# Second attention of a two-layer attention and expert program: the key-major scores from 32x128 stationary tiles

## What is computed

```
Q = query @ Wq + bq ; K = key @ Wk + bk ; V = value @ Wv + bv       (heads of 8 features)
Q = Q * cos + rotate_half(Q) * sin ; K = K * cos + rotate_half(K) * sin
scores = einsum('bhtd,bhsd->bhts', Q, K) / sqrt(8)
attn = softmax(scores, axis=-1)
context = einsum('bhts,bhsd->bhtd', attn, V) ; out = context @ Wo + bo
```

## Time and profile before

| | |
|---|---|
| median of 3 runs | 1782.54 us |
| lowest, highest | 1778.4, 1782.55 us |
| profiled execution, span from its first to its last instruction | 2270.0 us |
| a time of its own beside the span | the page gives none |
| busy: TensorE matmuls, VectorE, ScalarE, GpSimd | 1668.9, 1187.1, 941.9, 1124.3 us |
| mean granted TensorE clock | 0.830 |

### The profile page before, as it was taken

One profiled execution on the slowest core, in us unless ns is written; L12 is line 12 of the kernel. 1 busy time (PEld: TensorE's weight loads), 2 busy tenths in 40 slices (PEclk: granted clock), 3 DMA queues, 4 the chain that ended last, 5 costly groups with the idle time before them and its releaser, 6 DMA issues. The chain is left out here.

```text
span 2270.0 us, 58116 instructions
## 1 busy us (share of the span) xinstructions
PE 1668.9 (74%) x20814; PEld 1246.6 (55%) x20815; DVE 1187.1 (52%) x3485; ACT 941.9 (41%) x2258; POOL 1124.3 (50%) x1456
## 2 busy tenths in 40 slices
PE   6999993947877777826777767777855777777876
PEld 4777771437766677713444444444533555556654
DVE  5778777935555555623455455455666111222245
ACT  3777772723333333413334334344535233333322
POOL 4777761055555565464454454454212555555553
PEclk9999996967787777756888788778875898999888
DMA  4111110012323232521211111111000111111154
GB/s 169 44 42 36 41 30 13 1 44 77 82 77 79 77 85 78 75 59 63 84 41 37 34 40 36 34 39 37 24 14 15 37 40 37 41 40 40 39 143 140
DMA packets 136997, 122.89 MB, mean 54 GB/s; under 512 B 27675, under 2 KB 121915, under 8 KB 136123
## 3 DMA queue, kind: packets, MB, share of 16 engines
q0 software_dynamic: 26624, 56.35, 10.5%
q1 hardware_dynamic: 110078, 64.47, 9.3%
q10 hardware_dynamic: 192, 0.67, 0.1%
HBM read 80.24 MB, written 41.18 MB: 53 GB/s over the span
## 5 line engine op out<-in xcount | busy, mean ns | idle before, releaser
L1488 POOL DMA_INDIRECT arena<-expert_rows,token_of_slot x432 | 413.4, 957 | 402.0 <-issue 221.1
L419 POOL DMA_INDIRECT arena<-slot_results,slot x256 | 246.7, 964 | 118.5 <-issue 86.8
L1879 DVE TENSOR_TENSOR arena<-bank,arena 128x352 f32<-128x352 f32 x144 | 75.5, 524 | 354.3 <-ACT arena L1858 245.4
L1723 POOL DMA_INDIRECT token_results<-arena,slot x144 | 141.1, 980 | 189.9 <-DVE arena L1887 157.0
L909 PE MATMUL bank<-arena,Vp 128*32 128x64 f32 x4096 | 142.8, 230 | 114.6 <-issue 113.1
L1826 PE MATMUL bank<-W,arena 128*128 (+1 forms) x864 | 141.1, 305 | 108.9 <-ACT arena L1865 54.8
L1586 PE MATMUL bank<-arena 128*128 128x128 f32 x1152 | 195.7, 338 | 30.3 <-ACT arena L1633 12.7
L1826 PEld LDWEIGHTS bank<-W,arena 128*128 128x128 f32 (+1 forms) x864 | 127.2, 213 | 164.2 <-issue 156.7
L1812 PE MATMUL bank<-W,arena 128*128 x576 | 214.8, 500 | 1.7 <-ACT arena L1870 1.7
L1586 PEld LDWEIGHTS bank<-arena 128*128 128x128 f32 x1152 | 183.9, 249 | 39.7 <-issue 39.6
L619 DVE RECIPROCAL arena<-bank 128x256 f32<-128x256 f32 x64 | 112.1, 1752 | 173.6 <-PE bank L915 173.6
(11 more groups left out here) (215 smaller groups left out, 3622.8 us busy)
## 6 DMA issues: line engine op xcount, KB each, us to landing
slot_results<-arena SPq DMA_DIRECT2D x72, 256.0 KB
arena<-in_ctx SPq DMA_DIRECT2D x64, 128.0 KB
expert_rows<-arena SPq DMA_DIRECT2D x64, 128.0 KB
arena<-token_results SPq DMA_DIRECT2D x32, 256.0 KB
arena<-expert_rows,token_of_slot POOLq DMA_INDIRECT x432
W<-in_w SPq DMA_DIRECT2D x4, 1032.0 KB
X<-in_x SPq DMA_DIRECT2D x32, 128.0 KB, 2.1
arena<-slot_results,slot POOLq DMA_INDIRECT x256
```

The costliest lines, as they stand in the source:

```text
L419: nc.gpsimd.indirect_dma_start(out=gb[i.par][:, to:to + D], out_offset=None, in_=ys, in_offset=bass.IndirectOffsetOnAxis(ap=slot[:, at, k: ...
L1488: nc.gpsimd.indirect_dma_start(out=XE[n % R][:, c * ROW:(c + 1) * ROW], out_offset=None, in_=ts, in_offset=bass.IndirectOffsetOnAxis(ap=to ...
L1723: nc.gpsimd.indirect_dma_start(out=yt[half], out_offset=bass.IndirectOffsetOnAxis(ap=row_of_slot[:, at:at + 1], axis=0), in_=YE[n % 4][:, ...
```

## The change

In the second attention `turned` is replaced by `turned_pairs`. The block-diagonal keys, which exist already for `scores`, become the stationary operand: 32x128 tiles, two heads at once over all 128 output partitions, and 64 columns of the plain queries are the moving operand. This is again 32 matmuls. The maxima are subtracted by 32x128 slices of `max_to`, 256 columns of `mxT` as before, in 8 matmuls where there were 16. `Qbd` is no longer made or waited for. The first attention keeps `turned`; there, only conditions on `layer` that were always true or false are dropped.

```
-            Kbd, Qbd = carve2(1024), carve2(1024)
+            Kbd, Qbd = carve2(1024), None if layer else carve2(1024)
...
                             act.wait_ge(s["rope"], i.n + 1)
-                            for dst, src, done in ((Kbd, Kt, "kbd"), (Qbd, Qt, "qbd")):
-                                for j in range(4):
-                                    last = nc.scalar.activation(
-                                        dst[i.par].rearrange("p (b j k) -> p b j k", b=4, j=4)[:, :, j, :],
-                                        src[i.par].rearrange("p (b k) -> p b k", b=4), ACT.Copy,
-                                        scale=head_of[:, j:j + 1])
-                                last.then_inc(s[done], 1)
+                            for j in range(4):
+                                last = nc.scalar.activation(
+                                    Kbd[i.par].rearrange("p (b j k) -> p b j k", b=4, j=4)[:, :, j, :],
+                                    Kt[i.par].rearrange("p (b k) -> p b k", b=4), ACT.Copy,
+                                    scale=head_of[:, j:j + 1])
+                            last.then_inc(s["kbd"], 1)
...
+                    def turned_pairs(i):
+
+                        for sq in range(4):
+                            for j in range(2):
+                                for r in range(UNITS):
+                                    rows = slice(32 * r, 32 * r + 32)
+                                    nc.tensor.matmul(
+                                        U_[r][:, 128 * sq + 64 * j:128 * sq + 64 * j + 64],
+                                        Kbd[i.par][rows, 256 * sq + 128 * j:256 * sq + 128 * j + 128],
+                                        Qt[i.par][rows, 64 * sq:64 * sq + 64],
+                                        start=sq == 0 and j == 0, stop=False, skip_group_check=True)
+                        hold(pe, s["mx_here"], i.g + 1)
+                        for j in range(2):
+                            for r in range(UNITS):
+                                rows = slice(32 * r, 32 * r + 32)
+                                last = nc.tensor.matmul(
+                                    U_[r][:, :].rearrange("p (t j q) -> p t j q", t=4, j=2)[:, :, j, :],
+                                    max_to[rows, 2 * j * S:2 * (j + 1) * S],
+                                    mxT[rows, :].rearrange("p (t q) -> p t q", t=4),
+                                    start=False, stop=True, skip_group_check=True)
+                                if j == 1:
+                                    last.then_inc(s["t_psum"], 1)
...
                         if on(0):
                             maxima(i)
-                            turned(i)
+                            turned_pairs(i)
```

More of the change, by code:

```diff
@@ L869, in turned @@
                         hold(pe, s["qbd"], i.g + 1)
[L870 to L874, removed]
+                        for r, u in tiles_rb:
+                            rows = slice(32 * r, 32 * r + 32)
+                            nc.tensor.matmul(U_[r][64 * u:64 * u + 64, :], Mk[i.par][rows, 0:S], sel_of[rows, :],
+                                             start=True, stop=False, skip_group_check=True)
                         for sq in range(4):
@@ L883, in turned @@
                                     .rearrange("p (j u q) -> p j u q", j=2, u=2)[:, :, u, :],
-                                    start=bool(layer) and sq == 0, stop=False, skip_group_check=True)
+                                    start=False, stop=False, skip_group_check=True)
                         hold(pe, s["mx_here"], i.g + 1)
```

## The result

The changed kernel takes 1802.59 us (median of 4, 1797.48 to 1809.1) against 1782.55 us: a ratio of 1.0113, 95% interval 1.0083 to 1.0143. It is slower, by 20 us where 14 were forecast, and inside the range.

What follows compares the result with a forecast made beforehand. GpSimd was taken to bound gather steps at 13.1 us; the VectorE and TensorE loop would grow from 12.69 to 13.55, +0.45 times 27 = 12.2 us, plus 1.7 in closing steps: total +14, 1796 us, range 1777 to 1814.

Steps and rivals of the forecast that it cites:

- The pace of the wide tile: Key-major scores: 128-column load no longer hides under 64 moving columns; 16 x 0.110 = 1.76 us in place of 0.95.
- the ends of 0.94 and 2.70: Bounds for the wide scores group in us: load fully hidden, no change (0.94), or load and stream in turn (2.70).
- rival 3: Wide scores take load and stream in turn: 2.70 us, +1.75 a step, 1825 us in all; chance 0.07.
- The subtraction: Maxima subtracted after the scores: 16 instructions on four tiles keep the path's 1.1 us, change 0, bounds -0.1 and +0.1.
- the sum: Loop of VectorE and TensorE grows by 0.86 us, from 12.69 to 13.55; total +14 us.
- ScalarE's saving: Four Qbd activations fewer, -1.65 us of ScalarE's time: covered in gather steps, up to -0.28 us in closing steps.
- The bound of before: Gather steps of the second attention: GpSimd sets the step, by 0.4 us over the loop of VectorE and TensorE.
- The base of 13.1 us: Length taken for a gather step in the runs before the change; ends of 12.69 and 13.34 us.
- the closing steps: Five steps behind the last gather: 0.86 - 0.24 - 0.28 = +0.34 us each, 1.7 us in all.
- The lower clock: At 1.2 GHz 128 moving columns need as long as the load, so no cost; chance 0.22 together with rival 1.
- Against the profiled execution: Separate sum on the profiled span of 2270.0 us: 27 x (0.86 - 0.24) + 1.7 = +18, 2288 us.
- the standstill: TensorE idle in the values (L909) while GpSimd issues gathers; taken as in the profiled execution and mostly not the runs.

Runs made afterwards that it cites:

- b0: The kernel before, unchanged, run again for a second profile: 1784.13 us, ratio 0.9997.
- e5: The kernel before with only the subtraction of the maxima made wide (8 matmuls of 32x128), scores still narrow: 1780.97 us, ratio 0.9996.
- e6: The kernel before with the eight narrow score matmuls of the last sequence made twice: 1784.52 us, ratio 1.001.
- e9: The changed kernel with 96 of the 128 stationary columns in each score tile: 1792.65 us, ratio 1.0073.
- after: The changed kernel itself and its profile, against the kernel before: 1802.59 us, ratio 1.0113.
- e8: The changed kernel with 128 instead of 64 columns moving through each wide score tile: 1799.05 us, ratio 1.0102.
- e4: The changed kernel with the block-diagonal keys taken as 32x64 tiles (64 matmuls of 64 moving columns) and a narrow subtraction: 1808.14 us, ratio 1.0152.
- e3: The changed kernel with the subtraction of the maxima in the old narrow tiles (16 matmuls of 32x64): 1808.21 us, ratio 1.013.
- e7: The changed kernel with the wide score matmuls of the last sequence made twice: 1821.92 us, ratio 1.0229.
- e1: The changed kernel with Qbd still made by ScalarE and read by nobody: 1802.14 us, ratio 1.0091.
- e2: The kernel before with its narrow tiles but without Qbd, the block-diagonal keys read in its place: 1783.41 us, ratio 0.999.
- v1: The kernel before with GpSimd's two small products per step taken by ScalarE as four small activations: 1773.64 us, ratio 0.9963.
- v2: The kernel before with GpSimd's two small products and VectorE's copy of the gate logits both moved to ScalarE: 1773.59 us, ratio 0.996.

## Why the prediction was right, point by point

The mechanism held. Two of its sizes did not, and they partly cancelled, so that the forecast came closer than its terms. The table has, for each run, the distance from the start of the key-major scores to that of the projections, and the length of a step (from one L638 to the next), both as means from about 1000 to 1260 us, without the steps at a low granted clock and, for b0's distance, without the step of the late gather.

| run | two groups, us | step, us |
|---|---|---|
| b0 | 2.15 | 13.07 |
| e5, wide subtraction alone | 2.25 | 13.09 |
| e6, narrow group and a quarter | 2.44 | 13.28 |
| e9, 96 columns | 2.44 | 13.28 |
| after | 2.86 | 13.72 |
| e8, 128 columns moving | 2.86 | 13.71 |
| e4, 32x64 tiles of 64 columns | 2.98 | 13.85 |
| e3, wide scores, narrow subtraction | 2.99 | 13.84 |
| e7, wide group and a quarter | 3.31 | 14.15 |

From e6 on the step grows by what the two groups grow, whatever makes them longer: they lie on the loop that sets it. Above that, b0 and e5 stand at 13.07 and 13.09, where GpSimd holds the step.

- **The pace of the wide tile** was the step that decided: 16 x 0.110 = 1.76 us and 0.05 for the first load, 1.81 together, measured 1.84. Not the ends of 0.94 and 2.70. e8 excludes load and stream in turn (rival 3), e9 a fixed pace per tile. A rule that weight loads overlap only matmuls of another row group (the Trainium skill, "TensorE: Matmul & The Clock Gate", Part 3) would have made e8 27 us slower than after; it was not slower at all.
- **The subtraction** at 0: in the gather steps it was not. The projections start 1.03 us behind it in after and 1.15 in b0, and the narrow scores take 1.00 us there and not the 0.95 of a closing step. So the loop grew by 0.71 us where the sum had 0.86. Why the narrow groups vary from step to step was not tried. A change of width between the two groups costs 0.10 us (e3) or more (e5), a term that the sum did not have and did not need, because both groups have the same width.
- **ScalarE's saving** at nothing in gather steps: e1 and e2, from both sides.
- **The bound of before** was GpSimd: in b0 others wait for it and it waits for nobody. The base of 13.1 us was right (13.07), but its lead over the other loop was forecast at 0.4 us and is about 0.1: v1, with GpSimd out of the way, takes 12.96, and e6 gets 0.21 of its 0.29 us to show. The loop of VectorE and TensorE had been put at 12.69.
- **Sizes.** 0.86 added less 0.4 covered was 0.45 a step; 0.71 less some 0.1 is 0.65, as measured (13.72 - 13.07). Times 27 and with 0.8 for the closing steps (forecast 1.7) that is 18 us against 14. The profiled second attention has only 14.9 us, as good as the forecast, and that is luck: two of b0's steps stand at a low granted clock and are 3.8 us longer together, and none of after's is. The steps of after alternate: one with a wait of L852 of 0.77 us, the next with 0.58. The program's loop holds two steps, so its turn falls into every second; that this is the cause was not tried.
- **The 20 us of the medians**, with 18 from the steps, leave little open. Single executions of the changed kernel differ by more: 1797.48, 1799.67, 1805.51 and 1809.1 us, at mean granted clocks of 0.927, 0.928, 0.922 and 0.918, so the longer ones have the lower clock. Low stretches in the steps could do it (1.6 us each in e7), but this is not shown: e1's profiled execution is 4.9 us longer than after's with none, and 4.3 of them have passed before the first L638 (896.6 against 892.3). Nor do the profiles say what brings the stretches on. Between 1000 and 1300 us after, e1 and e8 have none, with the wide group; e7 has six, e9 five and e3 two; e4 has none; of the kernels with the narrow scores b0 has two, e2 and e5 one, and e6, v1 and v2 none.
- **The lower clock** the forecast had named only as a case in which the change would cost nothing. b0's narrow group at 0.50 bears that out for the group itself: 1.76 us to the subtraction, eight in sequence at 0.22 us each. That is the length of two wide loads, not of one as the forecast had it, which comes to the same, because the wide tiles are 16 in sequence. But a clock that falls for a few us also stretches the groups behind, in either kernel.
- **Against the profiled execution** the sum gave 2288 us, built on the standstill. The profiled execution after had none, so this number cannot be tested.

## What to carry to other kernels

In these groups a float32 matmul costs the longer of its stream and its weight load, as long as the number of instructions is not the limit (e4). With 64 moving and 128 stationary columns the load is the longer (0.115 against 0.059 us), and halving the stream while doubling the load was a loss even at the same number of instructions. Before pricing a change on one loop, look for an engine that never waits while others wait for it: here it was GpSimd, which hid about 0.1 us a step. Read the old length of a group in several steps of the stage that counts, not in one: here a single closing step gave 0.95 + 1.1 where the mean of the others was 2.15. When a profiled execution is much longer than the runs, look for a stretch that the runs cannot contain and take another profile before trusting its waits.

## What the runs showed of the hardware that was not expected

- The granted clock falls for a few us in the midst of steps of the unchanged kernel too. In b0 (a window as in e7's, and TensorE's timeline in it) it is 0.50, the lower level (1.2 of 2.4 GHz), and the narrow group then takes nearly as long as the wide one at the full clock, 1.76 us against 1.84:

```profile
1100.60:1104.00 3.40, 3.40 (x98) 2.57 (x96) 2.54 (x4) 0.69 (x3) 2.94 (x5) 0.50 0.15 39
```

```profile
1100.70 2.01 PE L878 MATMUL bank<-arena 32*64 32x128 f32 x64
1102.46 1.83 PE L890 MATMUL bank<-arena,fixed 32*64 32x256 f32 x32
```

- Narrow tiles with short streams (e4) do not come under 0.014 us for a load and its matmul over the whole group, so 128 of them took 1.80 us where loads and streams, as estimated for e4, would have allowed 0.9.
- Passing from 32x128 to 32x64 tiles between two groups of matmuls cost 0.10 us (e3), and from narrow to wide 0.09 to 0.22 (1.14 us in e5, 0.92 to 1.05 in b0).
- In every profile of the second attention but that of the standstill, two gathers some 190 us apart wait about 2 us with "issue" as the releaser (1.75 and 2.01 in b0, 2.15 and 2.17 in after). What they wait for is not in the profile.
- One profiled execution of the unchanged kernel took 490 us longer than b0's. In its second attention TensorE stood idle before L909 for 112.5 us, 232 times, with "issue" as the releaser, beside indirect DMAs. No other profile has this, and its cause stays open.
